# Selective scan: three, two, one, one groups of the state over PSUM in a block's four steps, each with one wide product and one wide copy

## The reference

```python
delta = jax.nn.softplus(x @ W_delta + b_delta)
Bm = x @ W_B + b_B
Cm = x @ W_C + b_C
A = -jnp.exp(A_log)
dA = jnp.exp(delta[..., None] * A)
dBx = delta[..., None] * Bm[:, :, None, :] * x[..., None]

def step(h, inputs):
    dA_t, dBx_t, C_t = inputs
    h = dA_t * h + dBx_t
    y_t = jnp.einsum('bdn,bn->bd', h, C_t)
    return (h, y_t)
```

## Time and profile before

| | before |
|---|---|
| median of 3 timed runs | 1099.65 us (1097.55 to 1106.23) |
| the profiled execution: its own time | 1094.59 us |
| its span in the profile | 1092.7 us |
| busy TensorE matmul, VectorE, ScalarE, GpSimd | 921.2, 669.3, 503.3, 294.6 us |
| the scan's steps 1 to 36 | 152 to 450 us in the profile |
| mean granted clock of TensorE | 0.924 of full speed |

### The profile page before, as it was taken

One profiled execution on the slowest core, in us unless ns is written; L12 is line 12 of the kernel. 1 busy time (PEld: TensorE's weight loads), 2 busy tenths in 40 slices (PEclk: granted clock), 3 DMA queues, 4 the chain that ended last, 5 costly groups with the idle time before them and its releaser, 6 DMA issues.

```text
span 1092.7 us, 17549 instructions
## 1 busy us (share of the span) xinstructions
PE 921.2 (84%) x5861; PEld 582.3 (53%) x5862; DVE 669.3 (61%) x1176; ACT 503.3 (46%) x1019; POOL 294.6 (27%) x357
## 2 busy tenths in 40 slices
PE   8997487877777777799999999999999996469996
PEld 6773443333323322346677777666667664336664
DVE  2533987988888988754554455477777773213332
ACT  1226577877779776343122222335444432323332
POOL 4922922333333310000000000074445410612222
PEclk9999768988999889999999999999999996579999
DMA  6282769453221212850411111000000002322220
GB/s 247 98 285 98 229 206 313 118 131 71 51 54 34 54 30 70 357 233 7 130 45 45 44 46 43 0 1 1 1 1 0 1 1 115 153 90 86 83 85 26
DMA packets 96258, 100.66 MB, mean 92 GB/s; under 512 B 64318, under 2 KB 81471, under 8 KB 94528
## 3 DMA queue, kind: packets, MB, share of 16 engines
q1 hardware_dynamic: 93456, 92.50, 26.7%
q0 software_dynamic: 2736, 7.30, 1.8%
HBM read 73.10 MB, written 39.18 MB: 103 GB/s over the span
## 4 chain that ended last, share of the span: by engine, by line
PE 64%; ACT 11%; DVE 10%; issue 7%; SPq 3%; DMA 3%; POOL 0%; ACTq 0%; DVEq 0%; POOLq 0%
PE ps L556 9%; PE ps L618 8%; PE ps L1228 6%; ACT mem L1659 5%; PE ps L1109 4%; PE ps L1518 4%; PE ps L1534 4%; PE ps L1431 3%; PE ps L1365 3%; PE ps L1188 3%; SPq L891 2%; PE ps L1387 2%; PE ps L1195 2%; ACT mem L1686 2%; DVE mem L2014 2%
## 5 line engine op out<-in xcount | busy, mean ns | idle before, releaser
L1066 POOL TENSOR_TENSOR mem<-mem,sm 128x296 f32<-128x296 f32 x128 | 87.2, 716 | 346.5 <-ACT mem L1754 306.4
L1659 ACT ACTIVATE mem<-ps 128x512 f32<-128x512 f32 x288 | 154.2, 629 | 24.0 <-PE ps L1188 12.9
L1044 POOL TENSOR_SCALAR mem<-mem,sm 128x16 f32<-128x16 f32 x148 | 105.4, 735 | 170.8 <-PE ps L1228 170.8
L556 PE MATMUL ps<-mem 128*128 (+1 forms) x384 | 110.2, 416 | 0.6 <-DVE mem L529 0.6
L1188 PE MATMUL ps<-mem 64*128 64x128 bf16 x1140 | 91.9, 232 | 20.6 <-ACT mem L1659 11.3
L1228 PE MATMUL ps<-mem 128*32 128x512 f32 x592 | 89.1, 675 | 22.3 <-issue 13.2
L1686 ACT ACTIVATE mem<-ps 128x512 f32<-128x512 f32 x148 | 82.3, 607 | 51.2 <-PE ps L1195 51.1
L1188 PEld LDWEIGHTS ps<-mem 64*128 64x128 bf16 x1140 | 56.4, 100 | 90.1 <-ACT mem L1659 69.4
L2014 DVE TENSOR_TENSOR mem<-mem 128x1024 f32<-128x1024 f32 x72 | 87.8, 1219 | 26.7 <-ACT mem L1659 26.7
L1195 PE MATMUL ps<-mem 64*128 64x512 bf16 x296 | 76.3, 424 | 31.5 <-DVE ps L2022 21.6
L2022 DVE TENSOR_TENSOR ps<-mem 128x512 f32<-128x512 f32 x144 | 93.6, 695 | 14.9 <-ACT mem L1686 14.3
(11 more groups left out here) (240 smaller groups left out, 1573.1 us busy)
## 6 DMA issues: line engine op xcount, KB each, us to landing
mem<-gates SPq DMA_DIRECT2D x7, 1184.0 KB, 6.0
mem<-in_w SPq DMA_DIRECT2D x2, 4096.0 KB, 16.3
slots<-mem SPq DMA_DIRECT2D x1, 6682.0 KB, 23.6
mem<-slots SPq DMA_DIRECT2D x26, 257.0 KB, 2.7
mem<-in_patches SPq DMA_DIRECT2D x7, 864.0 KB, 4.7
mem<-factor_rows SPq DMA_DIRECT2D x296, 16.0 KB, 1.8
mem<-factor_rows SPq DMA_DIRECT2D x37, 128.0 KB, 2.3
mem<-delta_rows SPq DMA_DIRECT2D x9, 512.0 KB, 4.5
```

Of the source, the lines that this page charges most:

```text
L556: mm = nc.tensor.matmul(ps[:, bank, 0:CH], w[:, k, row0:row0 + P], xn[:, k, cols], start=(k == 0), stop=(k == HALVES - 1))
L1044: nc.gpsimd.tensor_scalar(c_win4[:, t % SLOTS * 2 + r, :, w0:w0 + 8].rearrange("p j (x i) -> p j x i", i=2)[:, :, :, i], c_all[:, r * 16:r ...
L1659: nc.scalar.activation(decay_slots[b % 2][:, :, 4 * k:4 * k + 4], ps[:, ring_bank(at_), :].rearrange("p (e t) -> p t e", e=4), ACT.Exp).th ...
```

## The change

- Which groups go over PSUM now depends on the step (`grown_groups`): groups 1, 2 and 3 in the first step of a block, 1 and 3 in the second, only 1 in the third and fourth; and 1, 2 and 3 in all steps of the last block (t ≥ 33). All others are decay and add. Together 68 groups go over PSUM in t ≥ 1 instead of 72, 7 instead of 8 in a block, and 12 instead of 8 in the last block.
- A product into PSUM and a copy back are now one operation each over both banks, 1024 columns, and their semaphores rise by two at its end.
- The quads are handed out as 1, 8, 11 and 12 in the four steps of a block; before it was 2 in the first and about 10 in each other.
- The waits are counted with two tables, `ADDED_AT` and `GROWN_AT`, instead of by formulas.

```diff
         def quads_made(t, m):
 ...
-            u = (t - BLK * (b - 1) - 1) * GROUPS + m - 3
-            if u < 0:
-                return []
-            n = BLK * GROUPS - 3
-            return [(b, k) for k in range(QUADS * u // n, QUADS * (u + 1) // n)]
+            at_ = t - BLK * (b - 1) - 1
+            first, n = ((0, 1), (1, 8), (9, 11), (20, 12))[at_]
+            if at_ == 0:
+                return [(b, 0)] if m == 3 else []
+            return [(b, k) for k in range(first + n * m // GROUPS, first + n * (m + 1) // GROUPS)]
+
+        def grown_groups(t):
+            if t == 0:
+                return (1, 3)
+            if (t - 1) % BLK == 0 or t >= L - BLK:
+                return (1, 2, 3)
+            return (1, 3) if (t - 1) % BLK == 1 else (1,)
 ...
             def inject(t, m):
 ...
-                pe.wait_ge(added, 2 * t + m // 2)
+                pe.wait_ge(added, ADDED_AT[t, m])
 ...
             def grow(t, m):
 ...
-                        pe.wait_ge(seeded, 4 * (t - 1) + m - 1 + half + 1)
+                        pe.wait_ge(seeded, 2 * GROWN_AT[t, m] - 4 + half + 1)
 ...
             def copy_grown(t, m):
-                for half in range(2):
-                    act.wait_ge(grown, 4 * t + m - 1 + half + 1)
-                    quad = 2 * m + half
-                    nc.scalar.activation(slot[slot_of(t)][:, quad * 512:(quad + 1) * 512], ps[:, GROW_BANK + half, :],
-                                         ACT.Copy).then_inc(copied, 1)
+                act.wait_ge(grown, 2 * GROWN_AT[t, m] + 2)
+                nc.scalar.activation(slot[slot_of(t)][:, m * 1024:(m + 1) * 1024],
+                                     ps[:, GROW_BANK:GROW_BANK + 2, :].rearrange("p b n -> p (b n)"),
+                                     ACT.Copy).then_inc(copied, 2)
 ...
             def seed_state(t, m):
+                wait_state(t - 1, m)
                 now, before = slot[slot_of(t)], slot[slot_of(t - 1)]
-                for half in range(2):
-                    hs = slice((2 * m + half) * 512, (2 * m + half + 1) * 512)
-                    dve.wait_ge(copied, 4 * (t - 1) + m - 1 + 2 + half + 1)
-                    nc.vector.tensor_tensor(ps[:, GROW_BANK + half, :], now[:, hs], before[:, hs],
-                                            ALU.mult).then_inc(seeded, 1)
+                gs = slice(m * GW, (m + 1) * GW)
+                dve.wait_ge(copied, 2 * GROWN_AT[t, m] - 2 + 2)
+                nc.vector.tensor_tensor(ps[:, GROW_BANK:GROW_BANK + 2, :].rearrange("p b n -> p (b n)"),
+                                        now[:, gs], before[:, gs], ALU.mult).then_inc(seeded, 2)
 ...
             for t in range(L):
-                for m in range(0, GROUPS, 2):
-                    if t >= 1:
-                        decay_state(t, m)
-                        seed_state(t, m + 1)
-                    add_injected(t, m)
+                for m in range(GROUPS):
+                    by_pe = grown_groups(t)
+                    if m not in by_pe:
+                        if t >= 1:
+                            decay_state(t, m)
+                        if t >= 1 and m + 1 in by_pe:
+                            seed_state(t, m + 1)
+                        add_injected(t, m)
+                    elif t >= 1 and m - 1 in by_pe:
+                        seed_state(t, m)
```

More of the change, by code:

```diff
@@ L750, in quads_made, with added_to, grown_to @@
                 return []
-            u = (t - BLK * (b - 1) - 1) * GROUPS + m - 3
-            if u < 0:
-                return []
-            n = BLK * GROUPS - 3
-            return [(b, k) for k in range(QUADS * u // n, QUADS * (u + 1) // n)]
+            at_ = t - BLK * (b - 1) - 1
[9 more added lines that the diff above has]
+            return (1, 3) if (t - 1) % BLK == 1 else (1,)
+        ADDED_AT, GROWN_AT = {}, {}
+        for t in range(L):
+            for m in range(GROUPS):
+                if m in grown_groups(t):
+                    GROWN_AT[t, m] = len(GROWN_AT)
+                else:
+                    ADDED_AT[t, m] = len(ADDED_AT)
+        def added_to(t, m=GROUPS - 1):
+            return len([g for g in ADDED_AT if g <= (t, m)])
+        def grown_to(t, m=GROUPS - 1):
+            return len([g for g in GROWN_AT if g <= (t, m)])
         RING_AT = {}
@@ L883, in load_inject @@
                 if t >= INJ:
-                    sp.wait_ge(injected, 2 * (t - INJ + 1))
-                    sp.wait_ge(grown, 4 * (t - INJ + 1))
+                    sp.wait_ge(injected, added_to(t - INJ))
+                    sp.wait_ge(grown, 2 * grown_to(t - INJ))
                 n = t % INJ
@@ L940, in _ @@
             sp.dma_start(hF, h_dram).then_inc(kept_back, 16)
-            sp.wait_ge(multed, 2 * (L - BLK))
-            sp.wait_ge(seeded, 4 * (L - BLK))
+            sp.wait_ge(multed, added_to(L - BLK) - 2)
+            sp.wait_ge(seeded, 2 * grown_to(L - BLK) - 4)
             sp.wait_ge(read_ps, 2 * (L - BLK))
@@ L1048, in _ @@
                             S("c_half")[:, i:i + 1], None, ALU.mult).then_inc(window, 1)
-            pool.wait_ge(injected, 2 * L)
-            pool.wait_ge(grown, 4 * L)
+            pool.wait_ge(injected, added_to(L - 1))
+            pool.wait_ge(grown, 2 * grown_to(L - 1))
             nc.gpsimd.memset(xn[:, :, T:TP], 0.0).then_inc(zeros_set, 1)
@@ L1219, in read_state @@
                 first = r == 0 and (tp == 0 or t == 0)
-                pe.wait_ge(added, 2 * t + r + 1)
-                pe.wait_ge(copied, 4 * t + 2 * r + 2)
+                pe.wait_ge(added, added_to(t, 2 * r + 1))
+                pe.wait_ge(copied, 2 * grown_to(t, 2 * r + 1))
                 pe.wait_ge(window, 4 * t + 4)
@@ L1262, in _ @@
                 for m in range(GROUPS):
-                    if 1 <= t < L and m % 2 == 0:
+                    if 1 <= t < L and (t, m) in ADDED_AT:
                         inject(t, m)
-                    if 1 <= t < L and m % 2 == 1:
+                    if 1 <= t < L and (t, m) in GROWN_AT:
                         grow(t, m)
@@ L2005, in _, with wait_state @@
             GW = GP * P
+            def wait_state(t, m):
+                if m in grown_groups(t):
+                    dve.wait_ge(copied, 2 * GROWN_AT[t, m] + 2)
+                else:
+                    dve.wait_ge(added, ADDED_AT[t, m] + 1)
             def decay_state(t, m):
@@ L2031, in add_injected @@
                 else:
-                    dve.wait_ge(multed, 2 * (t - 1) + m // 2 + 1)
+                    dve.wait_ge(multed, ADDED_AT[t, m] - 2 + 1)
                     nc.vector.tensor_tensor(now, now, ps[:, INJ_BANK:INJ_BANK + 2, :], ALU.add).then_inc(added, 1)
             for t in range(L):
-                for m in range(0, GROUPS, 2):
-                    if t >= 1:
-                        decay_state(t, m)
-                        seed_state(t, m + 1)
-                    add_injected(t, m)
+                for m in range(GROUPS):
+                    by_pe = grown_groups(t)
[7 more added lines that the diff above has]
+                        seed_state(t, m)
             dve.wait_ge(kept_back, 16 * 4)
```

10 lines of the change are left out of this document (5 added, 5 removed).

## The result

The changed kernel takes 1145.34 us (median of 4 runs, 1142.62 to 1147.03); the kernel before took 1098.75 us beside it (4 runs, 1097.55 to 1106.23). The ratio is 1.0403, 95% interval 1.0372 to 1.0434: 4% slower. The sign was forecast; the size (+46.6 us against +22.3) lies above the range. Two later runs lie far off, one of 3700.64 us of e1 and one of 1278.64 us of e7, and are left out of the ratios.

What follows compares the result with a forecast made beforehand. VectorE was taken to limit each block's first step, ScalarE the other three. Blocks 1 to 7 add 13.3 us, the last 8.5, block 0 0.5: 22.3 on 1099.65 gives 1122 us, range 1107 to 1138.

Steps and rivals of the forecast that it cites:

- Durations of the fused operations: 1024-wide product into PSUM on VectorE 1.22 to 1.23 us; 1024-column copy back on ScalarE 1.05 us.
- The link: Fused product, matmuls, copy, then next product over the one pair of PSUM banks, in a row: 2.81 us.
- Rival 4: Links cost more: a 1.21 us copy makes a link 2.97 us, +7 us on the sum; chance 0.62 with the forecast.
- Order and walk: Step-by-step timing of operations through a block's four steps, ending at 33.9 us, 0.6 us more than 33.3.
- step 3: Third step of a block: product at 17.0 us from block start, then adds and decays, ending at 24.5 us.
- The clock term: TensorE at the lower clock around a block's first step: 0 to 2.7 us a block, half taken, 1.3 us.
- Rival 2: The low clock stays: 2.7 us in each block, more in the last, +38 in all, 1138 us; chance 0.12.
- The last block: Twelve links in a row, turns and some low clock: 36.4 us against 27.9, so 8.5 us more.
- Quads at no cost: Moved exponentials stay 32 a block; ScalarE's copies fall from 8.0 to 6.4 us; its fourth step holds 15 exponentials.
- Rival 3: ScalarE's relief decides: 32.6 us a block, 5 us gained against 7.5 lost in the last block, 1102 us; chance 0.12.
- Rival 1: The clock costs nothing: only 0.6 us a block and 7.5 us in the last block, +12, 1112 us; chance 0.14.
- What would show it: Expected signs: block starts about 35 us apart, first-step products 2.8 to 3.0 us apart, VectorE about 36 us in the last block.

Runs made afterwards that it cites:

- e1: Kernel before with only the fusion: one wide product and one wide copy a group, old groups and quads; 1095.19 us, ratio 0.9972.
- e7: Kernel before with only the new spread of quads (1, 8, 11, 12), 512 columns wide; 1107.41 us, ratio 1.0059.
- e6: Changed kernel with product and copy in halves of 512 and groups 1 and 3 in the last block; 1102.11 us, ratio 1.0029.
- e2: Changed kernel, same groups and quads, but product and copy in two halves of 512; 1112.21 us, ratio 1.0137.
- e3: Changed kernel, still fused, with only groups 1 and 3 over PSUM in the last block; 1122.93 us, ratio 1.0252.
- e4: Changed kernel plus filler matmuls, results unread, in each block's first step and all of the last block; 1123.55 us, ratio 1.0246.
- e10: e8 with product and copy fused except in t = 0, the blocks' first steps and the last block; 1099.78 us, ratio 1.0007.
- e8: Kernel before with only the new groups in blocks 0 to 7, 512 wide, old quads and last block; 1099.13 us, ratio 0.9986.
- e11: e10 plus one 256-column filler matmul behind the first growth in each block's first step and in the last block; 1095.40 us, ratio 0.9962.
- e9: e1 plus a 512-column filler matmul behind the first growth in each block's first step and in the last block; 1093.90 us, ratio 0.9962.

## Why the prediction was right and wrong

The regrouping's bill, in us of scan, from the runs:

| part | from | blocks 1–7, each | last block |
|---|---|---|---|
| new quads | before → e7 | +1.1 | 0 |
| three groups in the first step, 512 wide | e7 → e6 | −0.3 | |
| three groups throughout the last block, 512 wide | e7 → e2 | | +7.1 |
| fusing them | e6 → e3, e2 → after | +2.8 | +9.7 |
| sum | | +3.6 | +16.8 |

Seven times 3.6, and 16.8, make 42 of the 42.6 us. The row of the fusion has in it what its ring costs by way of the clock (e4).

- **Durations of the fused operations: right.** The product takes 1.232 us (1.22 to 1.23 forecast), the copy 1.030 (1.05). The section on the TRN2 errata of the page VectorE: DVE Perf Modes in the Trainium skill says larger tiles pay the fixed cost once; the product's busy time agrees (1.232 us for a pair's 1.30), and the kernel got slower all the same: the rule speaks of an engine's work and not of a ring's length. The 0.86 ns a column behind the copy's forecast is not the slope between its two widths (0.646 − 0.418 us over 296 columns, 0.77 ns); the copy itself shows 0.83.
- **The link: mechanism right, 0.14 us short.** The forecast had 0.43 us from the matmuls' start to the copy's; the rows of the last block have 0.52 (451.74 to 452.26). It had 1.10 from the copy's start to the next product; they have 1.15. 2.95 for 2.81, and 3.18 at the low clock. Rival 4's 2.97 was the right size, though not for its reason (the copy took 1.03 us, not 1.21).
- **Order and walk: right from step 3 on.** From the start of the block at 228.88, step 3's product stood at 19.9 us (17.0 forecast) and step 4's decay product at 27.1 (24.5). Steps 3 and 4 took 7.2 and 9.6 us against 7.5 and 9.4. The miss is all in steps 1 and 2, 2.9 us: 1.0 in step 1 from its three links, and 1.9 in step 2, from the turn (2.07 us) and the read (1.77 us) at half clock in the ring.
- **The clock term: the step that failed.** I priced it at up to 2.7 us a block and took half, 1.3. The block took 36.92 instead of 33.9 + 1.3 = 35.2. Against the walk's 33.9 the block was 3.0 us longer. Links of 2.95 us account for 0.4 of it (3 × 0.14); 2.6 us are left, all in steps 1 and 2, where the rows show matmul pairs of 0.61, a turn of 2.07 and a read of 1.77 us at half clock. Keeping part of the clock up gave 1.7 us back (e4). That the whole 2.6 is the clock's is argued from rows, the 1.7 is shown. Rival 2 had 2.7 us and 0.12 of the chance. Halving had no row behind it; the rows showed TensorE idle at a block's start, and the change made that idleness longer. That argued for the upper end.
- **The last block: the same step, larger.** From the decay product to the last read's start it is 42.9 us (449.31 to 492.25) against 27.9, +15.0; forecast +8.5, rival 2 +15. Three links are the long ones shown above; the eight others averaged 3.13 us, 2.5 us more than forecast together; the three, from a step's first product to its second in t = 34 to 36, took 13.6 us for 3 × 2.81 and 0.3 twice, another 4.6 over; I had 0.9 for all of the clock. Most of this is shown to be the clock's: in e4 the three take 9.6 us, and the last read starts 38.2 us from the decay product. Of the whole miss 12 × 0.14 = 1.7 us belong to the link at full clock. Against rival 2 I had argued that TensorE was busy two thirds of this block and its clock 0.94. That share was read from the kernel in which VectorE set the pace (it was busy 27.86 of 27.9 us there, against the prediction's sentence that in no block one engine is full): the ring left gaps of 2.57 us ahead of the matmuls, and the clock stayed at 0.50 for 30 us with TensorE busy 71% of them.
- **Quads at no cost: right within the walk, wrong as a reason.** The forecast's fourth step (ScalarE with 15 exponentials) came out. But e7 shows that this spread by itself costs 1.1 us a block, so it doesn't offset anything.
- **Rival 3 (ScalarE's relief) was small at best.** In e1 the blocks are the rival's 0.7 us shorter, but that has VectorE's shorter pair in it too, and in e10, with the new groups, the fusion of steps 2 to 4 shortened no block. With rings in the first step nothing of it is left to see: the wait for the last exponential fell to 1.14 us, but blocks grew.
- **Rival 1 (the clock costs nothing)** is excluded by e4.
- **What would show it.** Three products of a first step 2.8 to 3.0 us apart with VectorE idle: 2.95, and 3.18 at the low clock. Block starts 35 us apart: 36.9. Last block 36: 42.9. Wait at a block's start shorter than 3.13: 1.14. ScalarE idle ahead of the copies: 1.89 and 2.16.

What stays open: how much of the clock's loss remains in e4. It shortened the low level from 10.7 to 6.8 us in a block, no filler tried removed it, and the filler's own time (1.1 to 2.1 us of TensorE) is in its result. The last block with the old groups takes 31.3 us in before, e7, e8 and e11, and 32.6 to 32.8 in e1, e3, e6, e9 and e10. The traces explain this in part: in e1 and e10 the last turn of y takes 2.08 us, at the low clock, for 1.16 in the four; in e3, e6 and e9 VectorE waits once inside the block for a copy, 1.24, 0.61 and 1.24 us. The rest is open.

## What to carry to other kernels

Before fusing two halves of a hand-over between engines, ask whether anything else runs while it passes: with two products 3.4 us apart by VectorE's own work the fused link of 2.95 us was free and saved a little; with less work between them it was 1.07 us longer than the link in halves, and the gaps that it left cost more still by way of the clock. Count the links that the new order puts in a row, and price the clock with the gaps that the new order will have, not with the busy share of the old one. Where the new order makes a ring of three engines, work out the case in which all its matmuls, reads and turns run at the lower clock, and give it more than a small chance: here, with gaps of 2.57 us ahead of the matmuls, it was nearly what came.
